# Adding the causal triangle to a score tile: one product on 128 rows in place of two on 64 rows

## What is computed

```python
scores = jnp.einsum('bhqd,bhkd->bhqk', q, k) / math.sqrt(dk)
causal = jnp.tril(jnp.ones((T, T), dtype=bool))
scores = jnp.where(causal, scores, -jnp.inf)
attn = jax.nn.softmax(scores, axis=-1)
out = jnp.einsum('bhqk,bhkd->bhqd', attn, v)
```

## Time and profile before

| | |
|---|---|
| median of 3 runs | 2032.47 us (2029.73 to 2036.5) |
| the profiled execution: its time / its span | 2038.3 us / 2036.5 us |
| TensorE products busy / DVE / ACT | 1634.7 us (80%) / 1188.8 us (58%) / 956.1 us (47%) |
| mean granted TensorE clock | 0.885 |
| causal steps, second attention | about 621 to 876 us |
| causal steps, third attention | about 1068 to 1336 us |

### The profile page before, as it was taken

The page is one execution under the profiler, slowest core; times in us unless marked ns, Lnnn a source line. Parts: engine busy times, 40 slices in busy tenths (PEclk is TensorE's granted clock), DMA queues, the critical chain, the costliest instruction groups (busy, mean ns, idle before and its releaser), DMA issues. The chain is left out here.

```text
span 2036.5 us, 29639 instructions
## 1 busy us (share of the span) xinstructions
PE 1634.7 (80%) x10806; PEld 1010.4 (50%) x10806; DVE 1188.8 (58%) x2596; ACT 956.1 (47%) x1510; POOL 472.7 (23%) x546
## 2 busy tenths in 40 slices
PE   3899999869968999931069999968997799988576
PEld 1455555558855555510045555546775344433433
DVE  2576767443245665659855665635444676775375
ACT  1677879632314544510014444545764366566321
POOL 4220210022313213011033322004765323210100
PEclk8799999979977989975569999987998699999698
DMA  6241240010044345010154245020211454140322
GB/s 212 52 100 52 63 94 1 1 63 0 0 142 109 98 117 145 2 48 0 37 157 124 63 105 145 2 87 32 94 48 43 126 145 126 48 118 1 112 83 83
DMA packets 66899, 156.66 MB, mean 77 GB/s; under 512 B 9853, under 2 KB 15366, under 8 KB 65866
## 3 DMA queue, kind: packets, MB, share of 16 engines
q1 hardware_dynamic: 66762, 154.85, 27.3%
HBM read 105.39 MB, written 51.52 MB: 77 GB/s over the span
## 5 line engine op out<-in xcount | busy, mean ns | idle before, releaser
L984 DVE TENSOR_REDUCE a_mx<-PS 128x1 f32<-128x512 f32 (+3 forms) x768 | 395.3, 553 | 200.4 <-PE PS L1215 128.9
L1157 ACT ACTIVATE a_pT<-PS 128x1024 f32<-128x1024 f32 (+3 forms) x384 | 308.1, 811 | 221.4 <-PE PS L1239 155.1
L1210 PE MATMUL PS<-a_k,a_q 64*128 64x512 f32 (+3 forms) x768 | 246.5, 449 | 51.8 <-DVE a_mx L984 27.5
L361 DVE CUSTOM_DVE_ANT_0 PS<-PS,a_dist 128x448 f32<-128x448 f32 x256 | 155.1, 648 | 72.0 <-PE PS L592 71.0
L1230 PE MATMUL PS<-a_q,a_k 64*128 64x512 f32 (+3 forms) x768 | 180.0, 449 | 14.8 <-DVE a_q L989 6.1
L1253 PE MATMUL PS<-a_pT,a_va 128*32 128x512 f32 (+3 forms) x1536 | 170.2, 516 | 5.7 <-ACT a_raw L1113 5.7
L1210 PEld LDWEIGHTS PS<-a_k,a_q 64*128 64x128 f32 x768 | 115.4, 203 | 108.4 <-DVE a_mx L984 79.0
L492 ACT ACTIVATE a_p<-PS,a_negm 128x448 f32<-128x448 f32 (+1 forms) x256 | 149.2, 640 | 3.5 <-DVE a_negm L361 1.9
L602 PE MATMUL PS<-cst,a_p 128*128 128x128 f32 x1024 | 143.1, 282 | 4.4 <-ACT a_pT L500 1.9
L1230 PEld LDWEIGHTS PS<-a_q,a_k 64*128 64x128 f32 x768 | 79.5, 192 | 118.9 <-issue 91.6
L602 PEld LDWEIGHTS PS<-cst,a_p 128*128 128x128 f32 x1024 | 110.9, 142 | 38.2 <-issue 32.8
(11 more groups left out here) (337 smaller groups left out, 3451.0 us busy)
## 6 DMA issues: line engine op xcount, KB each, us to landing
spread_scratch<-a_high SPq DMA_DIRECT2D x96, 256.0 KB, 5.9
a_q<-spread_scratch SPq DMA_DIRECT2D x96, 256.0 KB, 5.6
a_k<-spread_scratch SPq DMA_DIRECT2D x96, 256.0 KB, 6.7
f_gb<-gate_rows SPq DMA_DIRECT2D x68, 256.0 KB, 5.3
spread_scratch<-a_low SPq DMA_DIRECT2D x48, 256.0 KB, 6.5
window_scratch<-a_high SPq DMA_DIRECT2D x24, 256.0 KB, 2.3
a_q<-window_scratch SPq DMA_DIRECT2D x32, 192.0 KB, 5.9
a_k<-window_scratch SPq DMA_DIRECT2D x32, 192.0 KB, 6.5
```

Source lines behind the costliest of these rows:

```text
L361: dve.tensor_tensor_reduce(PS[:, bank, 0:KW], PS[:, bank, 0:KW], dt_[:, off:off + KW], float(slopes[2 * pair + a]), 3e38, ALU.add, ALU.min ...
L984: dve.tensor_reduce(mx[:, gg % 2, qt, 2 * half + a:2 * half + a + 1], PS[:, 4 + a, 0:kw], AX.X, ALU.max).then_inc(max_done, 1)
L1157: act.activation(pT[:, N // 2 % 2, N % 2, :, q0:S], PS[:, 2 * (N % 2):2 * (N % 2) + 2, q0:S], ACT.Exp, scale=SCALE).then_inc(exp_done, 1)
L1210: mm = pe.matmul(ps[:, 0:kw], q[rows, b % 2, pair, qt * P:(qt + 1) * P], k[rows, b % 2, pair, 0:kw], start=True, stop=not causal)
```

## The change

The two products of a score tile become one: the whole identity (128 x 128) as stationary operand and the whole triangle as moving one, 128 columns wide, on all 128 rows. For it the input of masks gets 256 more columns, ACT converts them into a buffer of their own in each causal stage, and TensorE waits for both conversions. `scores_T` keeps its halves.

```diff
+        full_masks = sb("full_masks", [P, 2, P], BF16) if causal else None
...
-        masks_in = spare[:, KC * (WC + D):KC * (WC + D) + 6 * P]
+        masks_in = spare[:, KC * (WC + D):KC * (WC + D) + 8 * P]
...
-                    act.activation(half_masks[:, :, :, :].rearrange("p a b c -> p (a b c)"), masks_in,
+                    act.activation(half_masks[:, :, :, :].rearrange("p a b c -> p (a b c)"), masks_in[:, 0:6 * P],
+                                   ACT.Copy).then_inc(masks_done, 1)
+                    act.activation(full_masks[:, :, :].rearrange("p a b -> p (a b)"), masks_in[:, 6 * P:8 * P],
                                    ACT.Copy).then_inc(masks_done, 1)
...
                     if causal:
-                        pe.matmul(ps[:, kw - P:kw], half_masks[rows, 0, 0, :], half_masks[rows, 1, 0, :],
-                                  start=False, stop=False)
-                        mm = pe.matmul(ps[:, kw - 64:kw], half_masks[rows, 0, 1, :], half_masks[rows, 1, 1, 64:P],
-                                       start=False, stop=True)
+                        mm = pe.matmul(ps[:, kw - P:kw], full_masks[:, 0, :], full_masks[:, 1, :], start=False, stop=True)
                     mm.then_inc(s_done, 1)
...
-                    pe.wait_ge(masks_done, 1)
+                    pe.wait_ge(masks_done, 2)
...
-    return np.concatenate([halves, halves], 0).reshape(P, 6 * P).astype(np.float32)
+    halves = np.concatenate([halves, halves], 0).reshape(P, 6 * P)
+    return np.concatenate([halves, full[0], full[1]], 1).astype(np.float32)
```

## The result

The changed kernel takes 2112.6 us (median of 4 runs, 2107.2 to 2113.9) where the one before takes 2034.5 (4 runs). The medians lie 78 us apart; the ratio from the comparison of the runs is 1.035, with a 95% interval of 1.032 to 1.039. The forecast was 2136, in a range from 2085 to 2200. The profiled execution has a span of 2112.0 us against 2036.5, 75.5 us more.

The account below looks back on a forecast made before the run. TensorE was taken to set the pace in both causal attentions, with 38 us idle. Pairs +110 us, filled idle time -10, starts +4 gave +104 us: 2136 us against the median of 2032.5, range 2085 to 2200.

Parts of the forecast that it names:

- The bound: Steps of both causal attentions: TensorE sets the pace, busy 238.5 of 255 and 246.3 of 268 us.
- Pairs run together on the two halves of the rows: Causal score tiles: at full clock 124 pairs run together, 0.46 us, 86 apart, 0.80; with the change all run in series.
- The price of a switch: TensorE in score tiles: 0.09 us from 64-row to 128-row products, 0.10 us back, both in each tile.
- The pair: Two causal score tiles at full clock in the changed kernel: 0.51 us a tile, 1.02 us a pair, in series.
- 0.25 us of a tile's first product: Product of q and k in a tile's price: 0.235 us at mean 320 columns, 0.03 more for open load where hidden.
- 24 half-clock pairs: Step pairs at 1.2 GHz, 22 in the forecast: 1.68 us each in place of 0.67, together 22.2 us.
- the 0.80 us of the pairs apart: Kernel before, 86 full-clock pairs apart: mean from first start to next other product; going to 1.02 adds 18.9 us.
- The idle time: TensorE's 38 us idle in the steps: only 10.4 us, waits for the DVE's maxima, get filled; the rest left.
- the idle time takes more: Rival in the steps: maxima already pace pairs, 38 us idle fill first; +76, 2108 us; inside the forecast's 0.80 chance.
- The starts: Starts of the two causal stages, 24 pairs at half clock: 0.17 us more each, 4 us together.
- The masks: Larger mask load and ACT conversion, about 0.3 us a stage: free, since TensorE waits for k anyway.
- The clock: Rival: TensorE falls to 1.2 GHz in the steps, about +80 us on top, some 2215 us; chance 0.10.

Follow-up runs that it names:

- the series kernel: Kernel before with both tiles of a causal pair on partitions 0 to 63, so pairs run in series with no switch: 2082.3 us, 1.020 times.
- one-column product: Kernel before plus a 128-row product of zeros, one column wide, behind each causal score tile: 2213.6 us, four runs from 2175.2 to 2238.6.

## Why the prediction was right, and where it was off

**The bound** held for the changed kernel: TensorE is busy for 98% of its steps, and shorter maxima gain it next to nothing. For the kernel before the forecast read it too simply. TensorE's products cover 93% of its steps, but part of that is the second tile of a pair waiting for a maximum under the row of an earlier product, and a faster DVE alone gained 39 us. TensorE and the maxima set the pace there together.

**Pairs run together on the two halves of the rows, and stop doing so.** Shown: "x2" in the kernel before, none in the changed one, "x2" again when the products are grouped, with 40 to 50 us back. In the forecast I gave series and switches one common price; the series kernel shows that each is worth something like half. The rows that the forecast compared were of unlike tiles, 0.39 us for a pair of 256 columns and 1.13 for one apart of 512. Of 512 columns and up to `values`, together is 0.51 us, so the reading holds:

```profile
650.19 0.47 PE L1210 MATMUL PS<-a_k,a_q 64*128 64x512 f32 x2
...
650.70 0.85 PE L1253 MATMUL PS<-a_pT,a_va 128*32 128x384 f32 x8
```

The "x2" also says that TensorE's products do not start in the order of the program, though "The kernel before" says that they run in it. In the program all three products of tile a = 0 come ahead of those of a = 1; in the trace L1210 of both begins as one, ahead of either triangle. A product on the free half of the rows goes ahead of earlier ones on the other half, here even one of the next step's `scores_T` ahead of the last tile's triangle:

```profile
689.46 0.38 PE L1210 MATMUL PS<-a_k,a_q 64*128 64x256 f32 x1
689.47 0.50 PE L1230 MATMUL PS<-a_q,a_k 64*128 64x512 f32 x1
689.69 0.23 PE L1213 MATMUL PS<-a_half_masks 64*128 64x128 bf16 x1
```

**The price of a switch** held: 0.09 and 0.10 us forecast. In the changed kernel it is 0.23 us from L1213 to L1216 at 128 columns (849.11 to 849.34) where the forecast has 0.13 + 0.09, and 0.16 us from L1216 to the next, where it has 0.17. The one-column product shows 0.12 and 0.11 us. The figure of some 166 ns behind a product's columns, from "TensorE: Matmul & The Clock Gate" of the Trainium skill (Single matmul latency), would, as an estimate worked out from it, have made it 65 us more; no run shows that.

What counts as a switch was seen too narrowly. It is not only the number of rows: from the 128-row triangle to `values`, which is on 128 rows too but is 32 columns wide in the array (128*32), it is also 0.16 us (859.25 to 859.40, 0.159 in the median), and only to a product of the triangle's own shape (128*128) it is 0.04 to 0.07 us (857.52 to 857.59):

```profile
857.52 0.23 PE L1216 MATMUL PS<-a_full_masks 128*128 128x128 bf16 x1
857.59 0.61 PE L1261 MATMUL PS<-cst,a_m 128*128 128x128 f32 x4
...
859.25 0.23 PE L1216 MATMUL PS<-a_full_masks 128*128 128x128 bf16 x1
859.40 0.64 PE L1253 MATMUL PS<-a_pT,a_va 128*32 128x256 f32 x8
```

**The pair**: 1.02 us forecast, 0.965 measured. The forecast's 0.25 us of a tile's first product also stood between the 0.235 and the 0.265 that its words add up to. The two distances from L1213 to L1216 are 0.33 us each in the mean (0.34 forecast) and the one between the tiles 0.16 (0.17); the last one is 0.14 in the mean, because in about a third of the pairs the next product has the triangle's shape and no switch follows. 208 x 0.055 = 11 us too much. The 24 half-clock pairs cost 1.39 us in place of 1.68, 7 us too much; from L1216 to the next tile, where the forecast had 0.13 + 0.14, it is 0.22 us. And the 0.80 us of the pairs apart was counted to the first other product, which in 23 of the 232 pairs starts before the pair is through; so it was too short. In all, the time of the score tiles grew by 86 us (148.1 to 234.2) where the forecast had 110. This is the term that was off the most.

**The idle time** is the second one: "The other idle of the 38 us follows chains through ACT and POOL around TensorE's own turns, which are not shortened; I leave it." I let 10.4 us be filled; it was 28.0. The 38.2 us lie in three places: 10.6 us ahead of pairs, 11.8 ahead of the first product behind a pair, and 15.8 elsewhere. Now they are 0, 2.4 and 7.8. The first had been forecast. The second is inside the figures for a pair on both sides, so it must not be taken off again. The third fell by 8 us where I had left it, and that is the step that failed. It was not for the maxima: with short ones this part falls just as far, from 15.4 to 7.7 us. That TensorE has more of its own work to do while ACT and POOL run their chains, and so arrives later, fits this; no run changed the chains themselves.

Outside the score tiles the steps are 23 us shorter (374.7 to 351.9): 10.6 and 8.0 us of idle time, and 4 us more that is not idle. With the measured terms the sum is 86 - 23 + 4 = 67 us, as in the profile, against 104. The rival "the idle time takes more" came nearest with 2108 us, but not for its reason, that the maxima pace the pairs and only those together pay. Its sum keeps the 110 us of the pairs, 24 too much, and takes off 38 us of idle time where 23 went. The two errors largely cancel, and 7 us of the measured 78 are the fourth attention's, so its agreement with 2112.6 us is in part luck. The forecast's own 2136 us is held inside its range by a wide range more than by its sum, which is 104 us where 67 were measured in the same stages.

**The starts**: 1.9 us each, 4 us forecast together, 3.8 measured. **The masks**: nothing, as forecast.

**The clock** did not decide here, as forecast (0.91 and 0.94 in the steps); outside the two stages it gave 7 us that no step of the forecast had. In the one-column kernel it did: 335 us of its 710 in the steps were at 1.2 GHz in the longest run.

## What to carry to other kernels

A product that uses half of the rows is not half used if its partner for the other half follows at once: before making two narrow products into one wide one, look whether their rows in the timeline stand as "x2". A wide product between two narrow ones costs a switch on either side and the togetherness of both; if it must be, group products of one shape, rows and columns. When you price what surrounds a piece of work, count from start to start through to the end of the piece, and take each idle stretch off once. When work is added to the engine that sets the pace, any of its idle time may be filled, not only the waits for the engine that the change speeds up or slows down; when work is taken away, the idle time and a lower clock can take the gain back. And a high busy share does not say that an engine never waits: a short wait can lie under the row of the product before it, and only the faster other engine shows it.

## What the runs showed of the chip that was not expected

- 928 fewer products in 523 us of steps gained nothing: TensorE's time at 1.2 GHz rose from 59 to 116 us, its idle time from 38 to 52.
- Products on the two halves of the rows start out of the program's order: the second tile's product of q and k at 640.47 with the first tile's, ahead of both triangles.
- A switch of shape costs about 0.1 us, and from 128*128 to 128*32 as much as from 128*128 to 64*128 (0.16 us from the triangle's start, against 0.04 to 0.07 with no switch).
- A product of a single column on 128 rows behind each of 512 tiles on 64 rows cost 136 us in the shortest run and 200 in the longest, where 335 us of the steps were at 1.2 GHz; the same column on 64 rows cost nothing that can be told (1.002, 0.999 to 1.005).
- A stage that was the same in all kernels took 266 us with 11 us of it at 1.2 GHz, and 274 us with 33.
